# Attention layer on one core: the two small transfers of the row maxima issued by ScalarE instead of SyncE

## What is computed

```
q, k, v = x @ Wq[h] + bq[h], x @ Wk[h] + bk[h], x @ Wv[h] + bv[h]     # 16 heads, D = 16
scores  = einsum('bhtd,bhsd->bhts', q, k) * D ** -0.5
probs   = softmax(scores + causal, axis=-1)
x = layernorm(x + (probs @ v).reshape(B, T, 256) @ Wo + bo)
gate = silu((x @ fp8(gate_w)) * gate_scale);  up = (x @ fp8(up_w)) * up_scale
x = layernorm(x + ((gate * up) @ fp8(down_w)) * down_scale)
```

## Time and profile before

| | before |
|---|---|
| three timed runs, median | 549.65 us (548.6 to 552.53) |
| the profiled execution's own time | 551.15 us |
| its span, first to last instruction | 549.4 us |
| mean granted TensorE clock | 0.991 |
| busy share: PE, DVE, ACT, POOL | 96%, 83%, 58%, 41% |
| DMA: moved, mean over the span | 68.21 MB, 124 GB/s |

### The profile page before, as it was taken

How to read it: one execution, slowest core, us unless ns; L and a number is a source line. 1 busy time by engine, 2 the same in 40 slices (tenths; PEclk the granted TensorE clock), 3 DMA queues, 4 the chain that set the end, 5 groups by cost and what they waited for, 6 DMA issues and landing times.

```text
span 549.4 us, 10843 instructions
## 1 busy us (share of the span) xinstructions
PE 527.1 (96%) x3965; PEld 356.6 (65%) x3965; DVE 456.0 (83%) x815; ACT 318.1 (58%) x591; POOL 227.1 (41%) x258
## 2 busy tenths in 40 slices
PE   8979989999999999999999999998999999999994
PEld 3645446665666646656565665655578888888994
DVE  7886767898898889888888888999648888888886
ACT  3146676666676666766667666667554554345532
POOL 5013343253254335325424433523434653455453
PEclk9988999999999999999999999999999999999998
DMA  5864876567648466544864645620000101110112
GB/s 181 258 167 148 211 228 201 134 190 228 175 159 213 145 150 203 167 119 158 210 171 151 166 154 140 163 54 3 1 0 1 40 0 39 39 39 2 40 38 78
DMA packets 61549, 68.21 MB, mean 124 GB/s; under 512 B 6328, under 2 KB 55864, under 8 KB 61496
## 3 DMA queue, kind: packets, MB, share of 16 engines
q1 hardware_dynamic: 60664, 66.59, 42.3%
q10 hardware_dynamic: 832, 0.92, 0.5%
HBM read 37.62 MB, written 29.61 MB: 122 GB/s over the span
## 4 chain that ended last, share of the span: by engine, by line
PE 78%; DMA 8%; DVE 4%; issue 4%; ACT 3%; SPq 2%; POOL 1%; POOLq 0%; DVEq 0%; ACTq 0%
PE ps L1059 15%; PE ps L1011 11%; PE ps L1019 11%; PE ps L900 9%; PE ps L1179 8%; PE ps L992 6%; PE ps L969 5%; PE ps L993 4%; PE ps L908 4%; DMA q_st<-zero_rows 3%; PE ps L941 2%; DMA k_scratch<-part 2%; DMA m_scratch<-mrow 2%; PE ps L952 1%; ACT probs L471 1%
## 5 line engine op out<-in xcount | busy, mean ns | idle before, releaser
L648 DVE TENSOR_REDUCE nmax<-ps 128x2 f32<-128x1024 f32 (+1 forms) x192 | 196.5, 1039 | 49.9 <-PE ps L993 49.3
L471 ACT ACTIVATE probs<-ps 128x512 f32<-128x512 f32 x320 | 184.1, 597 | 74.5 <-PE ps L1011 73.1
L392 POOL TENSOR_SCALAR_AFFINE_SELECT probs<-probs 128x512 f32<-128x512 f32 x128 | 86.1, 686 | 204.9 <-ACT probs L471 204.9
L1011 PE MATMUL ps<-q_st,k_st 98*128 98x384 bf16 (+3 forms) x512 | 122.0, 302 | 4.9 <-ACT probs L471 3.7
L420 POOL TENSOR_TENSOR f_l<-f_full,f_h 128x512 fp32r<-128x512 f32 (+1 forms) x54 | 64.4, 1196 | 73.6 <-ACT f_h L557 73.4
L992 PE MATMUL ps<-k_st,q_st 98*128 98x256 bf16 (+2 forms) x384 | 82.0, 274 | 5.5 <-DMA k_st<-k_scratch 2.2
L993 PE MATMUL ps<-k_st,q_st 124*128 124x128 bf16 x512 | 84.1, 221 | 0.0
L1019 PE MATMUL ps<-probs,v_st 128*32 128x512 f32 (+3 forms) x1024 | 82.5, 438 | 0.6 <-POOL probs L392 0.6
L1011 PEld LDWEIGHTS ps<-q_st,k_st 98*128 98x128 bf16 x512 | 44.0, 98 | 49.8 <-issue 26.9
L550 ACT ACTIVATE sgate<-ps,s_gate 128x512 f32<-128x512 f32 (+1 forms) x54 | 34.2, 638 | 59.9 <-PE ps L1059 59.9
L993 PEld LDWEIGHTS ps<-k_st,q_st 124*128 124x128 bf16 x512 | 46.0, 98 | 18.4 <-DVE nmax L648 13.7
(11 more groups left out here) (100 smaller groups left out, 841.1 us busy)
## 6 DMA issues: line engine op xcount, KB each, us to landing
q_st<-q_scratch SPq DMA_DIRECT2D x31, 384.0 KB
k_st<-k_scratch SPq DMA_DIRECT2D x31, 384.0 KB
q_scratch<-part SPq DMA_DIRECT2D x16, 384.0 KB, 2.6
k_scratch<-part SPq DMA_DIRECT2D x16, 384.0 KB, 2.6
xT<-in_attn_xT SPq DMA_DIRECT2D x8, 512.0 KB, 3.9
q_scratch<-part SPq DMA_DIRECT2D x16, 256.0 KB, 2.9
resid<-in_attn_x SPq DMA_DIRECT2D x8, 512.0 KB, 5.9
k_scratch<-part SPq DMA_DIRECT2D x15, 256.0 KB, 2.1
```

The source lines that it names most:

```text
L392: pool.affine_select(out=blocks, in_=blocks, compare_op=ALU.is_ge, fill=0.0, base=0, pattern=[*pattern, [1, P]], channel_multiplier=-1).th ...
L471: act.activation(probs[:, u, :], ps[:, u % 2, :], ACT.Exp, scale=SCALE).then_inc(exp_done, 1)
L648: dve.tensor_reduce(nmax[:, i, heads[0]:heads[-1] + 1], src, AX.X, ALU.max, negate=True).then_inc(max_taken, 1)
L1011: m = pe.matmul(ps[:, u % 2, c0:c0 + T - P * j], k_st[0:RP, g, h, P * j:P * j + P], q_st[0:RP, g, h, P * j:T], start=True, stop=True)
```

## The change

`store_mrow` and `load_mrow` leave SP's program and are written into ScalarE's. In ScalarE's group w they serve group w+1: the store stands behind the copy `yT` and ahead of the 5th exp, the load behind the 8th exp. Both keep their waits, and the load gets one more, for the slot's stack (`stack_loaded`), which includes the zeros that it overwrites; on SP the order of issue stood for that with the wait for the store. The group-0 maxima of block 0 take another way and are untouched.

```diff
@@ sync: helpers @@
-            def store_mrow(n, g):
-                sp.wait_ge(mT_out, n * G + g + 1)
-                sp.dma_start(m_scratch[g].rearrange("i a h p -> (i a h) p"), mrow[0:TB * RM * HG, :]).then_inc(mrow_stored[g], 16)
-
-            def load_mrow(n, g):
-                sp.wait_ge(mrow_stored[g], (n + 1 if g else n) * 16)
-                sp.dma_start(q_st[0:RM, g].rearrange("a h (i p) -> a h i p", i=TB),
-                             m_scratch[g].rearrange("i a h p -> a h i p")).then_inc(mrow_loaded[g], 16)
@@ sync: the loop over blocks @@
                 load_stack(n, 3)
-                store_mrow(n, 1)
-                load_mrow(n, 1)
...
-                store_mrow(n, 2)
-                load_mrow(n, 2)
...
-                store_mrow(n, 3)
-                load_mrow(n, 3)
...
                 if nxt:
-                    store_mrow(n + 1, 0)
-                    load_mrow(n + 1, 0)
                     load_stack(n + 1, 2)
@@ scalar @@
+            def store_mrow(w):
+
+                act.wait_ge(mT_out, w + 1)
+                act.dma_start(m_scratch[w % G].rearrange("i a h p -> (i a h) p"), mrow[0:TB * RM * HG, :]).then_inc(mrow_stored[w % G], 16)
+
+            def load_mrow(w):
+                n, g = w // G, w % G
+
+                wait(act, stack_loaded[g], stack_count(n, g))
+                act.wait_ge(mrow_stored[g], (n + 1 if g else n) * 16)
+                act.dma_start(q_st[0:RM, g].rearrange("a h (i p) -> a h i p", i=TB),
+                              m_scratch[g].rearrange("i a h p -> a h i p")).then_inc(mrow_loaded[g], 16)
...
                     if w:
                         empty_y(w - 1)
+                    if w + 1 < W:
+                        store_mrow(w + 1)
                     exps(w, 4)
...
                     exps(w, 7)
+                    if w + 1 < W:
+                        load_mrow(w + 1)
                     if split:
                         hi_part(n + 1, g + 1)
```

## The result

| | before | after |
|---|---|---|
| timed runs, median | 549.21 us (548.6 to 552.53, 4 runs) | 581.82 us (574.35 to 584.65, 4 runs) |
| profiled execution's own time, span | 551.15, 549.4 us | 583.78, 582.0 us |
| mean granted TensorE clock | 0.991 | 0.966 |
| PE busy | 527.1 us | 538.2 us |

The change makes the kernel slower. The ratio is 1.0504 (95% interval 1.0447 to 1.0561). The prediction said 554.0 us, 547 to 559, so the time lies far outside its range.

What follows compares the result with a forecast made beforehand. TensorE, busy 96% of the span, was taken as the bound. Removed waits -3.0, ScalarE's issues 0 and loads behind SP's traffic +7.8 gave +4.8 us: 554.0 us from a median of 549.65, range 547 to 559.

Steps and rivals of the forecast that it cites:

- What bounds the kernel: Whole kernel: TensorE is busy 96% of the span, so a change pays or costs only where TensorE stands still.
- The gain of 3.0 us: TensorE's waits on zero rows and maxima's rows go once SP no longer stops at store and load: -3.0 us.
- ScalarE's issue costs nothing: ScalarE's queue gets 31 store and 31 load issues, which hold up no exp that matters: 0, upper bound 3.4 us.
- rival 2: ScalarE issues only when its engine is empty: +3.4 us for the store, each load 0.6 us later; 559 us, chance 0.17.
- Blocks 3 to 6, "0.9 us to spare": Blocks without w_raw: the load, behind stack and x, lands at 308.2 against 309.10, 0.9 us before TensorE wants it.
- Block 0, 3.0 us: Load behind stack and x: TensorE waits 1.7 us, or 4.4 if w_raw's issue comes first; the middle, 3.0.
- Blocks 1 and 2, 2.2 and 2.1 us: Loads behind stack 2, x and w_raw, in block 1 also the scales: TensorE waits 2.2 and 2.1 us.
- The other groups, 0.5 us: At most one 776 KB stack or 768 KB of parts ahead, 0 to 1 us to spare; 0.5 us for misses.
- TensorE's clock, nothing: No TensorE clock below the earlier 0.99 expected, as waits of 2 us were there before without one.
- Rival 1: Served in turn: ScalarE's transfers pass SP's backlog and the load lands within 3 us of the 8th exp; 547.0 us, chance 0.25.
- rival 3: Nothing moves: the stack waits stay, hanging on the parts' landing, and the load just makes it; 549.7 us, chance 0.08.

## Why the prediction was wrong

**The mechanism was right, its size was not, and the clock was left out by a misreading.** The load stands behind SP's issued transfers, SP issues earlier because nothing stops it, and waits stand at groups 4, 8 and 12. With x and what follows it held back three quarters of the loss go, with more traffic it grows. The steps in order:

- *What bounds the kernel.* Right: every us here is one of TensorE standing, or running at the lower clock.
- *The gain of 3.0 us.* Right in kind, and where it was seen alone near its size: no wait on the zero rows, group 4 1.44 us shorter at full clock, group 14 1.2 us (12.39 to 11.19).
- *ScalarE's issue costs nothing.* Right for the exps: the store's issue (324.11, 0.36 us) ran beside yT (324.10), and the exp followed 0.50 us after yT's start, as in the earlier trace rows. The 3.4 us of rival 2 are not there. But I had looked only at who waits for the issue, not at what the issue waits for. It comes after yT's wait for TensorE, and in steady blocks that lets stack 2 go first.
- *Blocks 3 to 6, "0.9 us to spare".* This step failed. It let the load go with the 8th exp and looked only at the traffic ahead of the load. The store has to land first, and it too stood behind stack 2. At group 24 the load went out 329.40 - 327.46 = 1.94 us late, and took 5.02 us where the sum gave it 2.9 (from 3.8 us before the score to 0.9 before it). 1.94 + 2.1 - 0.9 = 3.1 us, and 3.07 were measured. Groups 24, 28 and 20 together: 7.6 us against nothing.
- *Block 0, 3.0 us.* I had the case that came, w_raw's issue ahead of the load's, at 4.4 us, and took the middle. It was 5.05.
- *Blocks 1 and 2, 2.2 and 2.1 us.* 2.91 and 3.93. At group 8 the load went out 0.51 us behind the 8th exp, again for the store's landing; from issue to score it took 6.33 us, against the 5.96 of the sum.
- *The other groups, 0.5 us.* 4.8 us, of which 2.35 at group 2. There stacks 0 and 1 and x go out from 51.84 to 55.08, more than the one stack that I took to be ahead.
- *TensorE's clock, nothing.* This step failed too and cost about 11 us in the profiled execution. The argument was that waits of 2 us had been there before without a fall, and that is not so: the longest wait in its table, 2.15 us for k_st at the start, was followed by a clock of 0.50. Its row, and the window behind it:

```profile
36.91 0.32 PE L992 MATMUL ps<-k_st,q_st 98*128 98x384 bf16 x1 [2.15 <-DMA k_st<-k_scratch]
...
38.00:43.50 5.50, 5.12 (x19) 2.68 (x18) 2.88 (x4) 2.77 (x7) 1.79 (x2) 0.50 0.42 114
```

  Read rightly, that row gave the three forecast waits of 2 to 3 us a possible price in clock, and the sum had none. In after, waits of 1.1 to 1.4 us left the clock alone, and each of the six for maxima from 2.35 to 5.05 us came with a stretch at 0.50 and a longer group behind it.

With the gain as predicted and the two losses as measured: -3.0 + 24.3 + 11.1 = +32.4 us, against 32.6 in the span. That this comes so near is in part luck, since the gain was measured in waits alone (1.9 us on the zero rows, 0.5 at group 5) and smaller changes cancel. Rival 1 (served in turn, 547) is refuted by stores of 5.2 us and loads of 5.0, rival 2 by the exps on time, rival 3 by the zero rows. The forecast itself counted on issue order, and the store of group 24 took 2.8 us more than that gives.

**Still open:** how the DMA engines choose between two queues, why the store's last packets came so late, and what decides whether a wait brings the clock down. I did not try to let SP hold stack 2 itself until the store has landed, with both transfers on ScalarE; that would bring back the brake that the change took away.

## What to carry to other kernels

A wait in a queue of transfers is also a brake: it keeps bulk traffic from getting ahead of a small urgent transfer. Before you take it away, write down for every small transfer what will be issued ahead of it afterwards, for both legs of a store-and-load pair, and hold back by a semaphore whatever isn't urgent. A dependent load belongs on a queue whose engine has nothing else to do: behind a wait on ScalarE stand the exps. And where the bottleneck is TensorE, read from the trace before what the clock did after each wait, and price a new wait with a slower clock behind it as well: here that was 11.1 us on top of 24.3 us of waits.

## What the runs showed of the hardware that I had not expected

- A DMA issue on ScalarE runs entirely beside a running activation: 324.11 for 0.36 us beside yT from 324.10 for 0.60 us, and the next exp begins at 324.60.
- 8 KB cost 1.3 us at best and up to 5.4 us behind SP's transfers when ScalarE issues them (landings 1.3/2.0/5.4 us, min/median/max over 31); on GpSimd's queue 1.6/1.7/5.4.
- A wait for data of 5.05 us cost TensorE another 2.1 us behind it (13.70 against 11.59 us for group 4), and keeping it at work with 20 useless matmuls gave those back.
